# A decoder's routed experts on chosen tokens only: rows scattered by expert, computed in blocks behind the loop, gathered back

## Chip, cores and metric

One core of one Trainium2 chip. The metric is the device time of one execution in microseconds; lower is better. All data are float32 unless a line says otherwise.

## What is computed

Four sequences of 512 tokens of width 256 pass six stages, A to F, each `x = x + stage(layernorm(x))`: five attention layers and, last, the mixture of experts (F), which the change rewrites:

```python
B, S, D_MODEL = 4, 512, 256
E, H, I, G, TKG, TOPK, NSH = 32, 256, 128, 8, 4, 8, 2
scores = sigmoid(h @ gate_w.T); sc = scores + gate_bias
group_scores = top_k(sc.reshape(-1, G, E // G), 2)[0].sum(-1)
masked = where(group in the TKG best, sc, 0); tki = top_k(masked, TOPK)[1]
tkw = take(scores, tki); tkw = tkw / (tkw.sum(-1) + 1e-20) * 2.5
combine = (one_hot(tki, E) * tkw[..., None]).sum(1)          # (tokens, E), 8 of 32 not zero
g = silu(einsum('th,eih->tei', h, w_gate)); u = einsum('th,eih->tei', h, w_up)
routed = einsum('tei,ehi->th', g * u * combine[:, :, None], w_down)
shared = silu(h @ sh_gate.T) * (h @ sh_up.T) @ sh_down.T      # two more experts for all tokens
x = x + routed + shared
```

## The kernel before

The program has a setup and then a loop of four rounds, one per sequence. Each engine has an instruction list of its own; a round runs stages A to F with a barrier of all engines behind each (`Steps.end`), and `end_round` clears the semaphores. x stays in SBUF as four tiles of 128 tokens by 256; SyncE stores it at the end of the round (L2006). TensorE runs warm-up matmuls (`keep_warm`, L412) where it would wait: twelve in front of F's barrier, eight behind.

Stage F (`f_pe`, `f_act`, `f_dve`, `f_sp`) computes all 32 experts for all 512 tokens, with the shared experts as numbers 0 and 1. Per expert `up` (L1257) is four matmuls of 512 columns into two PSUM banks, and `down` (L1286) four of 256 columns that accumulate in banks 6 and 7 over all 34 experts. A float32 matmul stands in the trace as two instructions. Between them ScalarE takes the SiLU (L1332) and VectorE multiplies by the up half (L1378, L1380) and by the token's routing weight (L1387). The routing weights are made by VectorE in `gate` (L1341 to L1371), turned by TensorE and copied through DRAM as one broadcast row per expert (`load_row`, L1223, its source stored at L1230). SyncE loads the experts' weights, 384 KB each, in a ring of six (L1236), and after the sixth the next round's x and the weights of stage A (`load_ahead`, L1215 to L1217). At expert 14 VectorE takes the statistics of the next round's x (L352) and normalises it (L366) in place of `xn`; at experts 18 and 19 TensorE turns it (`next_pe`). At the end VectorE adds banks 6 and 7 to x (L1401).

Of the kernel before, what the change touches and what calls it, by code (L numbers as in the profile page):

```python
# [16 lines left out]
I32 = mybir.dt.int32  # L17
ALU = mybir.AluOpType
# [3 lines left out]
P = 128  # L22
# [168 lines left out]
NRING = 6  # L191
F_ROWS = 4
# [29 lines left out]
def decoder(nc, io, out, rounds=B):  # L222
    ctx = ExitStack()
    with ctx:
# [38 lines left out]
        selE = sb("selE", [96, NE, P], BF16)  # L263
# [23 lines left out]
        x_stored = ctx.enter_context(nc.semaphore("x_stored"))  # L287
        dve_chain = sem("dve_chain")
# [70 lines left out]
        def ln_scaled(dve, ch, rows, powered, n, done):  # L359
# [5 lines left out]
            for i in range(NI):  # L365
                nc.vector.tensor_scalar(xn[:, i, :], rows(i), mv[:, i, 0:1], rstd[:, i:i + 1],  # L366
                                        ALU.subtract, ALU.mult).then_inc(done, 1)

# [30 lines left out]
        def next_pe(pe, k, bank):  # L399
            pe.wait_ge(next_xn, NI)  # L400
            for i in range(NI):
                last = nc.tensor.transpose(ps[:, bank, i * P:(i + 1) * P], xn[:, i, k * P:(k + 1) * P], ident[:, :])
            last.then_inc(next_tr, 1)
# [764 lines left out]
        named("F", "lg_mm", "lg_exp", "comb", "ct_mm", "ct_up", "gu_mm", "silu", "gu", "down")  # L1168

        if "F" in STAGES:  # L1170
            w_in = [sem(f"w_in{k}_F") for k in range(NRING)]


        row_in = [setup_loaded, setup_dve, setup_pool_sem, setup_act]

        F_DIRECT = [NSH, NSH + 1]
        rows_kept = nc.dram_tensor("weight_rows", (NE, S), F32, kind="Internal").ap()

        def row_of(e):

            return ctxT[:, e % F_ROWS // 2, e % 2 * S:(e % 2 + 1) * S]

        F_NEXT_LN = 14
        F_NEXT_T = range(18, 20)

        def f_mem(sb2):
            m = {}
            m["w"] = sb2("f_w", [P, NRING, 3 * DM])
# [4 lines left out]
            m["t8"] = sb2("f_t8", [P, NI, 8])  # L1193
            m["m4"] = sb2("f_m4", [P, NI * 8, 4])
# [5 lines left out]
            m["rest"] = sb2("f_rest", [P, NI, NE])  # L1200
            m["cp"] = sb2("f_cp", [P, NI, 3, NE], BF16)
            m["cT"] = sb2("f_cT", [96, S], BF16)
            m["rows"] = sb2("f_rows", [NE, S])
            m["si"] = sb2("f_si", [P, 2, S])
            m["gu"] = sb2("f_gu", [P, 2, S])
            m["tm"] = sb2("f_tm", [P, S])
# [994 lines left out]
```

## Time and profile before

| | |
|---|---|
| three timed runs, us | 4085.89, 4087.71, 4091.82 (median 4087.71) |
| the profiled execution: span from first to last instruction, us | 4082.7 |
| TensorE / VectorE / ScalarE / POOL busy, us | 3805.6 / 2426.6 / 1752.6 / 152.0 |
| mean granted clock of TensorE | 0.987 |
| DMA: moved, mean rate | 286.26 MB, 70 GB/s |

The page and the trace give the profiled execution's time as its span, 4082.7 us, and no other time of it. An engine's busy time counts no waiting, no register work and no issuing of DMAs. PE is TensorE's matmul side, PEld its weight loads, DVE VectorE, ACT ScalarE, POOL GpSimd, SPq SyncE's queue. A matmul's end is modelled and includes its way through the array, so the distance between starts says what one costs. The granted clock is given in parts of 2.4 GHz.

### The profile page before, as it was taken

The numbers are of one execution on the slowest core, as the hardware profiler recorded it, in microseconds if no ns is written. First come the engines' busy times: TensorE is split into PE (matmuls) and PEld (weight loads), VectorE is DVE, ScalarE is ACT, GpSimd is POOL, SyncE is SP. The second block draws the span as 40 slices with busy tenths as digits, with TensorE's granted clock in tenths as the row PEclk, the third lists the DMA queues.
The fourth block names the chain that finished last, engine by engine and source line by source line (L and its number), as shares of the span: only waits on it lengthen the run. The fifth ranks groups of instructions, "written<-read, shape, count | busy, mean of one in ns | idle before, by whom it ended". The sixth has DMA issues, their size and how long they took to land.

```text
span 4082.7 us, 59517 instructions
## 1 busy us (share of the span) xinstructions
PE 3805.6 (93%) x22502; PEld 1826.4 (45%) x22502; DVE 2426.6 (59%) x6081; ACT 1752.6 (43%) x3256; POOL 152.0 (4%) x168
## 2 busy tenths in 40 slices
PE   4999899999999989999999998999999999899999
PEld 2353444345435244435544524443553443444355
DVE  5568576843366856683237676767333776676642
ACT  1755434531274643462128374336113836433611
POOL 1000020000000002000000001100000000200000
PEclk9999999999999999999999999999999999999999
DMA  5313002133331200203342210130435121012043
GB/s 174 128 43 63 19 17 52 25 111 127 115 119 34 54 19 24 57 13 129 128 137 90 40 38 19 44 50 1 148 109 163 63 52 26 19 46 48 1 164 98
DMA packets 152763, 286.26 MB, mean 70 GB/s; under 512 B 25317, under 2 KB 84709, under 8 KB 147557
## 3 DMA queue, kind: packets, MB, share of 16 engines
q1 hardware_dynamic: 152456, 282.22, 24.1%
q8 instruction: 186, 3.05, 0.3%
q14 instruction: 121, 0.98, 0.1%
HBM read 187.49 MB, written 44.30 MB: 57 GB/s over the span
## 4 chain that ended last, share of the span: by engine, by line
PE 76%; DVE 17%; ACT 4%; issue 2%; PEldq 1%; SPq 0%; DMA 0%; PEld 0%; DVEq 0%; POOLq 0%; ACTq 0%
PE ps L1257 11%; PE ps L589 7%; PE ps L572 6%; PE ps L1286 5%; PE ps L412 5%; DVE mx L755 4%; PE ps L516 4%; PE ps L1676 3%; PE ps L1573 3%; PE ps L577 3%; PE ps L1614 3%; PE ps L468 2%; PE ps L1597 2%; DVE ps L752 2%; PE ps L620 2%
## 5 line engine op out<-in xcount | busy, mean ns | idle before, releaser
L693 ACT ACTIVATE PT<-ps 128x512 f32<-128x512 f32 (+2 forms) x1280 | 643.8, 564 | 324.5 <-PE ps L577 174.7
L1257 PE MATMUL ps<-xnT,f_w 128*128 128x512 f32 x1088 | 489.7, 593 | 0.0
L755 DVE TENSOR_REDUCE mx<-ps 128x1 f32<-128x512 f32 (+3 forms) x768 | 430.7, 617 | 75.4 <-PE ps L516 38.3
L572 PE MATMUL ps<-QS,KS 99*128 99x512 bf16 (+2 forms) x1280 | 419.0, 368 | 9.2 <-ACT PT L693 8.7
L516 PE MATMUL ps<-KS,QS 96*128 96x512 bf16 (+3 forms) x1280 | 391.6, 367 | 17.4 <-DVE mx L755 6.9
L752 DVE CUSTOM_DVE_ANT_0 ps<-ps,mneg 128x512 f32<-128x512 f32 x512 | 340.7, 718 | 82.2 <-PE ps L516 79.1
L589 PE MATMUL ps<-PT,VP 128*32 128x512 f32 (+3 forms) x2560 | 371.1, 573 | 0.0
L412 PE MATMUL ps<-mneg,identb 128*128 128x512 bf16 x1200 | 314.6, 388 | 28.9 <-DVE a_fin L1791 10.9
L1380 DVE TENSOR_TENSOR f_tm<-f_si,ps 128x512 f32<-128x512 f32 x128 | 88.0, 687 | 426.2 <-ACT f_si L1332 425.9
L1332 ACT ACTIVATE f_si<-ps 128x512 f32<-128x512 f32 x136 | 81.3, 597 | 584.2 <-PE ps L1257 584.2
L1257 PEld LDWEIGHTS ps<-xnT,f_w 128*128 128x128 f32 x1088 | 205.5, 190 | 201.4 <-issue 195.2
L572 PEld LDWEIGHTS ps<-QS,KS 99*128 99x128 bf16 x1280 | 108.5, 97 | 390.9 <-ACT PT L693 237.3
L1286 PE MATMUL ps<-f_w,f_gu 128*128 128x256 f32 x1088 | 258.3, 380 | 7.2 <-DVE f_gu L1387 7.2
L1286 PEld LDWEIGHTS ps<-f_w,f_gu 128*128 128x128 f32 x1088 | 205.7, 190 | 93.3 <-issue 59.4
L1791 DVE TENSOR_TENSOR a_fin<-a_fin,ps 128x512 f32<-128x512 f32 (+1 forms) x176 | 104.5, 635 | 208.8 <-PE ps L1656 207.4
L516 PEld LDWEIGHTS ps<-KS,QS 96*128 96x128 bf16 x1280 | 127.5, 100 | 222.5 <-DVE mx L755 73.9
L682 ACT ACTIVATE QS<-ps 3x512 bf16<-3x512 f32 x192 | 113.1, 589 | 225.6 <-PE ps L554 222.5
L1756 ACT ACTIVATE a_X<-ps,b1A 128x1024 f32<-128x1024 f32 (+2 forms) x152 | 169.2, 1156 | 72.1 <-PE ps L1620 71.5
L577 PE MATMUL ps<-mnegT,identb 128*128 128x512 bf16 x512 | 194.6, 380 | 0.0
L412 PEld LDWEIGHTS ps<-mneg,identb 128*128 128x128 bf16 x1200 | 113.1, 100 | 157.5 <-issue 23.2
L775 DVE RECIPROCAL rq<-ps 128x16 f32<-128x16 f32 x48 | 12.4, 257 | 224.8 <-PE ps L526 224.8
L1732 ACT ACTIVATE a_fin<-ps 128x2048 f32<-128x2048 f32 (+1 forms) x64 | 79.2, 1237 | 153.1 <-PE ps L1597 152.4
(282 smaller groups left out, 5584.1 us busy)
## 6 DMA issues: line engine op xcount, KB each, us to landing
f_w<-in_wF SPq DMA_DIRECT2D x136, 384.0 KB, 3.1
ctxT<-weight_rows SPq DMA_DIRECT2D x120, 256.0 KB, 3.4
scores<-a_fin SPq DMA_DIRECT2D x64, 256.0 KB, 3.0
a_fin<-scores SPq DMA_DIRECT2D x32, 512.0 KB, 4.3
a_Y<-in_wA SPq DMA_DIRECT2D x5, 3072.0 KB, 14.7
KS<-KP SPq DMA_DIRECT2D x240, 64.0 KB, 2.3
scores<-a_fin SPq DMA_DIRECT2D x64, 192.0 KB, 3.0
a_fin<-scores SPq DMA_DIRECT2D x12, 1024.0 KB, 7.6
```

The costliest lines, as they stand in the source:

```text
L412: nc.tensor.matmul(ps[:, bank, :], identb[:, :], mneg[:, 0, 0:BANK], start=True, stop=True)
L516: last = nc.tensor.matmul(o, m["QS"][0:KR, h, i * P:(i + 1) * P], m["KS"][0:KR, h, f:f + w], start=True, stop=not c.causal)
L572: last = nc.tensor.matmul(o, m["KS"][0:KST, h, j * P:(j + 1) * P], m["QS"][0:KST, h, q0:S], start=True, stop=plain)
L577: last = nc.tensor.matmul(o, identb[:, :], mnegT[:, j, :], start=False, stop=True)
L589: last = nc.tensor.matmul(ps[r:r + 32, 6, q0:S], m["VP"][:, j, h, :], m["PT"][:, mp % 2, j % 2, e, 0:S - q0], start=(j == 0), stop=(j == c ...
L693: nc.scalar.activation(m["PT"][:, mp % 2, j % 2, e, 0:w], ps[:, SLOTS + n % TURNED, 0:w], ACT.Exp, scale=HD ** -0.5).then_inc(g("exp"), 1)
L752: nc.vector.tensor_tensor_reduce(ps[:, k % SLOTS, 0:w], ps[:, k % SLOTS, 0:w], mneg[:, i, f:f + w], 1.0, NEG, ALU.add, ALU.max, m["mx"][:, ...
L755: nc.vector.tensor_reduce(m["mx"][:, h % 2, i, f // BANK:f // BANK + 1], ps[:, k % SLOTS, 0:w], AX.X, ALU.max, negate=True).then_inc(g("sl ...
L1257: last = nc.tensor.matmul(ps[:, 2 * v + e % 2, :], m["w"][:, e % NRING, (2 * v + k) * P:(2 * v + k + 1) * P], xnT[:, k, :], start=(k == 0) ...
L1286: last = nc.tensor.matmul(ps[:, 6 + i // 2, (i % 2) * DM:(i % 2 + 1) * DM], m["gu"][:, e % 2, i * P:(i + 1) * P], m["w"][:, e % NRING, 2 * ...
L1573: last = nc.tensor.matmul(ps[:, 4 + e % 4, :], m["w"][:, k, col:col + P], xnTA[:, k, :], start=(k == 0), stop=(k == KD - 1))
L1756: nc.scalar.activation(m["hid"][k % 2][:, n * x:n * x + n, 0:w], ps[:, A_UP + n * x:A_UP + n * x + n, 0:w], ACT.Gelu, bias=b1A[:, 0:1]).th ...
```

## The change

In the loop, F computes the gate and the two shared experts only. `chosen` (0 or 1) is counted over the tokens by small bf16 matmuls (`ranks`), so that each chosen (token, expert) pair has a slot: expert number times `ROOM` plus its rank. x with the shared experts added goes to DRAM (`x_kept_rows`); keys and weights of all rounds stay in `hist`. Behind each round's end POOL scatters the 512 normalised rows, eight times each, into `slot_rows` in DRAM. The next round's x is normalised into a buffer of its own (`xnA`) so that `xn` stays for the scatter.

Behind the loop stand new programs of all engines. All 32 experts' weights (12.6 MB) are loaded into SBUF, the tail of each expert's slots is filled with zero rows, and a table of 159 blocks of 128 slots (4 x 512 x 8 pairs, rounded up by expert) is made. Each block is loaded, turned, multiplied with its expert's weights, chosen by a register, and stored. Then POOL gathers each token's eight rows back, and VectorE adds them up with their weights.

```diff
-            for e in range(NE + NSH):
...
-                sp.dma_start(MF["w"][:, e % NRING, :], io["wF"][e]).then_inc(w_in[e % NRING], 16)
-                if e == NRING - 1:
-                    load_ahead(sp, b + 1, ahead)
...
+            for e in range(NSH):
+                sp.dma_start(MF["w"][:, e, :], io["wF"][e]).then_inc(w_in[e], 16)
+            load_ahead(sp, b + 1, ahead)
             sp.wait_ge(ahead, 3 * 16)
...
+            def ranks():
+                pe.wait_ge(g("chosen"), 1)
+                for i in range(NI):
+                    for j in range(i + 1):
+                        nc.tensor.matmul(ps[:, 4, i * NE:(i + 1) * NE], earlierb[:, :] if j == i else onesb[:, :], m["cb"][:, j, :],
+                                         start=(j == 0), stop=(j == i))
+                for i in range(NI):
+                    last = nc.tensor.matmul(ps[:, 4, NI * NE:(NI + 1) * NE], onesb[:, :], m["cb"][:, i, :], start=(i == 0), stop=(i == NI - 1))
+                last.then_inc(g("rank_mm"), 1)
             up(0)
             up(1)
             pe.wait_ge(x_kept, n)
             down(0)
             down(1)
+            ranks()
+            next_pe(pe, 0, 5)
+            next_pe(pe, 1, 1)
...
+            for r in range(B - 1):
+                ch.link(nc.vector.tensor_copy(hist[:, :, NI * r:NI * (r + 1), :], hist[:, :, NI * (r + 1):NI * (r + 2), :]))
...
+            ch.link(nc.vector.tensor_tensor(f2("rp"), f2("rp"), f2("mb"), ALU.is_lt))
+            nc.vector.tensor_copy(m["cb"][:, :, :], f2("rp")).then_inc(g("chosen"), 1)
+            dve.wait_ge(ahead, 3 * 16)
+            ln_stats(ch, lambda i: M1["x"][:, i, :], next_var)
+            ch.link(nc.vector.tensor_tensor(f2("mb"), f2("rp"), f2("sc"), ALU.mult))
...
+            ln_scaled(dve, ch, lambda i: M1["x"][:, i, :], next_pow, 0, next_xn, m["xnA"])
+            dve.wait_ge(g("down"), NSH)
...
+            ch.link(nc.vector.tensor_tensor(key, key, f2("rp"), ALU.mult))
+            for i in range(NI):
+                last = nc.vector.max(m["p8"][:, i, :], hist[:, 0, NI * (B - 1) + i, :])
+            ch.link(last)
+            ch.link(nc.vector.tensor_scalar(slot8[:, :, :], m["p8"][:, :, :], -1.0, None, ALU.add))
...
+        def to_slots(pool):
+            for i in range(NI):
+                for k in range(TOPK):
+                    nc.gpsimd.indirect_dma_start(out=slot_rows, out_offset=bass.IndirectOffsetOnAxis(ap=slot8[:, i, k:k + 1], axis=0),
+                                                 in_=xn[:, i, :], in_offset=None).then_inc(scattered, 16)
...
+        RX, RT, RH, RY, RG = 4, 3, 3, 4, 8
+        NT = B * NI
+        AHEAD_T, AHEAD_U = 3, 2
...
+        def g_sp(sp):
+            for q in range(8):
+                sp.dma_start(m["W"][:, 4 * q:4 * q + 4, :], io["wF"][NSH + 4 * q:NSH + 4 * q + 4].rearrange("e p c -> p e c")).then_inc(g("W_in"), 16)
+            sp.wait_ge(x_stored, 16)
+            sp.dma_start(m["acc"], x_kept_rows.rearrange("b (t p) d -> p (b t) d", p=P)).then_inc(g("kept_in"), 16)
+            sp.wait_ge(g("ends"), 1)
+            for e in range(NE):
+                end = sp.value_load(ends[0:1, e:e + 1], min_val=ROOM * e, max_val=ROOM * e + TOKENS)
+                sp.dma_start(slot_rows[bass.ds(end, P), :], zeros[:, :]).then_inc(g("padded"), 16)
+            sp.wait_ge(g("tables"), 1)
+            sp.wait_ge(scattered, 16 * B * NI * TOPK)
+            sp.wait_ge(g("padded"), 16 * NE)
+            by_block = slot_rows.rearrange("(a p) d -> a p d", p=P)
+            def load(b):
+                if b >= RX:
+                    sp.wait_ge(g("xt_mm"), b - RX + 1)
+                first = sp.value_load(table[b % P:b % P + 1, 1, b // P:b // P + 1], min_val=0, max_val=NE * ROOM // P - 1)
+                sp.dma_start(m["xb"][:, b % RX, :], by_block[bass.ds(first, 1), :, :].rearrange("o p d -> p (o d)")).then_inc(g(f"x_in{b % RX}"), 16)
+            for b in range(RX):
+                load(b)
+            for b in range(NBLOCK):
+                if b + RX < NBLOCK:
+                    load(b + RX)
+                sp.wait_ge(g("y_up"), b + 1)
+                sp.dma_start(block_out[b * P:(b + 1) * P, :], m["y"][:, b % RY, :]).then_inc(g(f"y_out{b % RY}"), 16)
...
+        def g_pool(pool):
+            pool.wait_ge(g("rows8"), 1)
+            for r in range(RY):
+                pool.wait_ge(g(f"y_out{r}"), y_stored(r))
+            for t in range(NT):
+                if t >= RG:
+                    pool.wait_ge(g("summed"), t - RG + 1)
+                for k in range(TOPK):
+                    nc.gpsimd.indirect_dma_start(out=MG["back"][:, t % RG, k, :], out_offset=None, in_=block_out,
+                                                 in_offset=bass.IndirectOffsetOnAxis(ap=rows8[:, t, k:k + 1], axis=0)).then_inc(g(f"back{t % RG}"), 16)
...
+        def g_pe(pe):
+            def turn_x(b):
+                pe.wait_ge(g(f"x_in{b % RX}"), 16 * (b // RX + 1))
+                if b >= 2:
+                    pe.wait_ge(g("xt_up"), b - 1)
+                for k in range(KD):
+                    last = nc.tensor.transpose(ps[:, b % 2, k * P:(k + 1) * P], m["xb"][:, b % RX, k * P:(k + 1) * P], ident[:, :])
+                last.then_inc(g("xt_mm"), 1)
+            def up(b, e):
+                pe.wait_ge(g("xt_up"), b + 1)
+                if b >= 2:
+                    pe.wait_ge(g("hid"), b - 1)
+                for k in range(KD):
+                    last = nc.tensor.matmul(ps[:, 2 + b % 2, 0:2 * P], m["xT"][:, b % RT, k, :],
+                                            m["W"][:, bass.ds(e, 1), 2 * P * k:2 * P * (k + 1)].rearrange("p o c -> p (o c)"),
+                                            start=(k == 0), stop=(k == KD - 1))
+                last.then_inc(g("gu_mm"), 1)
+            def turn_h(b):
+                pe.wait_ge(g("hid"), b + 1)
+                if b >= 2:
+                    pe.wait_ge(g("ht_up"), b - 1)
+                nc.tensor.transpose(ps[:, 4 + b % 2, 0:P], m["h"][:, b % RH, :], ident[:, :]).then_inc(g("ht_mm"), 1)
+            def down(b, e):
+                pe.wait_ge(g("ht_up"), b + 1)
+                if b >= 2:
+                    pe.wait_ge(g("y_up"), b - 1)
+                nc.tensor.matmul(ps[:, 6 + b % 2, 0:DM], m["hT"][:, b % 2, :], m["W"][:, bass.ds(e, 1), 2 * DM:3 * DM].rearrange("p o c -> p (o c)"),
+                                 start=True, stop=True).then_inc(g("y_mm"), 1)
...
+            pe.wait_ge(g("W_in"), 8 * 16)
+            pe.wait_ge(g("tables"), 1)
+            for b in range(-AHEAD_T, NBLOCK):
+                if b + AHEAD_T < NBLOCK:
+                    turn_x(b + AHEAD_T)
+                if b >= 0:
+                    turn_h(b)
+                if 0 <= b + AHEAD_U < NBLOCK:
+                    u = b + AHEAD_U
+                    expert[u] = pe.value_load(table[u % P:u % P + 1, 0, u // P:u // P + 1], min_val=0, max_val=NE - 1)
+                    up(u, expert[u])
+                if b >= 0:
+                    down(b, expert.pop(b))
...
+        def g_act(act):
+            for b in range(-AHEAD_T, NBLOCK):
+                t, u = b + AHEAD_T, b + AHEAD_U
+                if t < NBLOCK:
+                    act.wait_ge(g("xt_mm"), t + 1)
+                    if t >= RT:
+                        act.wait_ge(g("gu_mm"), t - RT + 1)
+                    nc.scalar.activation(m["xT"][:, t % RT, :, :], ps[:, t % 2, 0:DM].rearrange("p (k c) -> p k c", k=KD), ACT.Copy).then_inc(g("xt_up"), 1)
+                if b >= 0:
+                    act.wait_ge(g("ht_mm"), b + 1)
+                    if b >= 2:
+                        act.wait_ge(g("y_mm"), b - 1)
+                    nc.scalar.activation(m["hT"][:, b % 2, :], ps[:, 4 + b % 2, 0:P], ACT.Copy).then_inc(g("ht_up"), 1)
+                if 0 <= u < NBLOCK:
+                    act.wait_ge(g("gu_mm"), u + 1)
+                    if u >= 2:
+                        act.wait_ge(g("hid"), u - 1)
+                    nc.scalar.activation(m["si"][:, u % 2, :], ps[:, 2 + u % 2, 0:P], ACT.Silu).then_inc(g("silu"), 1)
...
+        def g_dve(dve):
...
+            for b in range(-AHEAD_U, NBLOCK):
+                u = b + AHEAD_U
+                if u < NBLOCK:
+                    dve.wait_ge(g("silu"), u + 1)
+                    if u >= RH:
+                        dve.wait_ge(g("ht_mm"), u - RH + 1)
+                    nc.vector.tensor_tensor(m["h"][:, u % RH, :], m["si"][:, u % 2, :], ps[:, 2 + u % 2, P:2 * P], ALU.mult).then_inc(g("hid"), 1)
+                if b >= 0:
+                    dve.wait_ge(g("y_mm"), b + 1)
+                    if b >= RY:
+                        dve.wait_ge(g(f"y_out{b % RY}"), 16 * (b // RY))
+                    nc.vector.tensor_copy(m["y"][:, b % RY, :], ps[:, 6 + b % 2, 0:DM]).then_inc(g("y_up"), 1)
+            dve.wait_ge(g("kept_in"), 16)
+            for t in range(NT):
+                dve.wait_ge(g(f"back{t % RG}"), 16 * TOPK * (t // RG + 1))
+                for k in range(TOPK):
+                    ins = nc.vector.scalar_tensor_tensor(out=m["acc"][:, t, :], in0=m["back"][:, t % RG, k, :], scalar=weight8[:, t, k:k + 1],
+                                                         in1=m["acc"][:, t, :], op0=ALU.mult, op1=ALU.add)
...
         @block.gpsimd
                 st.end_round()
+                to_slots(pool)
+            g_pool(pool)
```

In setup, the table `selE` of POOL goes; two small loads and four fills or copies of VectorE come in.

## Rows read from the trace of the kernel before

**Rows 1.** Busy time of the engines, and the chain that ended last, by engine (the page)

```profile
PE 3805.6 (93%) x22502; PEld 1826.4 (45%) x22502; DVE 2426.6 (59%) x6081; ACT 1752.6 (43%) x3256; POOL 152.0 (4%) x168
...
PE 76%; DVE 17%; ACT 4%; issue 2%; PEldq 1%; SPq 0%; DMA 0%; PEld 0%; DVEq 0%; POOLq 0%; ACTq 0%
```

**Rows 2.** The page's costliest groups, the two of the expert matmuls

```profile
L1257 PE MATMUL ps<-xnT,f_w 128*128 128x512 f32 x1088 | 489.7, 593 | 0.0
...
L1286 PE MATMUL ps<-f_w,f_gu 128*128 128x256 f32 x1088 | 258.3, 380 | 7.2 <-DVE f_gu L1387 7.2
```

**Rows 3.** The chain in order of time, first round, stage F: start us, us, what

```profile
906.04 3.43 PE ps L1257 x8
909.48 1.73 PE ps L1286 x8
```

**Rows 4.** Timeline of stage F, first round: start us, us, instructions [idle before <- releaser]

```profile
864.81 2.71 SPq L1236 DMA_DIRECT2D f_w<-in_wF  x6
...
869.53 1.04 PE L418 MATMUL ps<-ident,xn 128*128 128x128 f32 x8
...
874.12 0.23 DVE L1341 TENSOR_SCALAR f_sc<-f_sc 128x128 f32<-128x128 f32 x1 [3.06 <-ACT f_sc L1319]
...
885.54 0.29 DVE L1360 TENSOR_TENSOR f_rp<-f_rp,f_mb 128x128 f32<-128x128 f32 x1
...
887.25 0.23 DVE L1366 TENSOR_SCALAR f_mb<-f_mb 128x128 f32<-128x128 f32 x1
...
947.77 1.41 DVE L352 BATCH_NORM_STATS2 st<-a_Y 128x6 f32<-128x256 f32 x4
...
1053.70 4.73 PE L412 MATMUL ps<-mneg,identb 128*128 128x512 bf16 x20
1053.97 1.28 DVE L1401 TENSOR_TENSOR x<-x,ps 128x512 f32<-128x512 f32 x2 [2.16 <-PE ps L1286]
```

**Rows 5.** DMA issues: what, engine, count, KB each, median us to landing

```profile
f_w<-in_wF SPq DMA_DIRECT2D x136, 384.0 KB, 3.1
...
KS<-KP SPq DMA_DIRECT2D x240, 64.0 KB, 2.3
...
scores<-a_fin SPq DMA_DIRECT2D x64, 128.0 KB, 2.5
...
wbuf<-in_woA SPq DMA_DIRECT2D x5, 1024.0 KB, 17.1
...
weight_rows<-f_rows SPq DMA_DIRECT2D x4, 64.0 KB, 1.6
```

**Rows 6.** Busy time by stretch, DMA share and GB/s at the right

```profile
874.00:884.00 10.00, 10.00 (x28) 5.12 (x27) 9.29 (x20) 2.57 (x4) 0.00 (x0) 1.00 1.03 409
```

**Rows 7.** SyncE's issues: line, duration ns min/median/max, first and last start

```profile
L1230 SPq DMA_DIRECT2D weight_rows<-f_rows x4: 325/325/330, 892.6 to 3913.2; - x4
...
L2006 SPq FUSED_REGOPS  x4: 42/43/43, 1058.5 to 4079.2; - x4
...
L2006 SPq DMA_DIRECT2D out<-x x4: 404/404/405, 1058.7 to 4079.4; - x4
```

**Rows 8.** Small reads of PSUM and SBUF, by line: duration ns min/median/max

```profile
L424 ACT ACTIVATE xnT<-ps x40: 592/597/619, 301.8 to 3891.8; 128x512 f32<-128x512 f32 x40
...
L366 DVE TENSOR_SCALAR xn<-ps,mv,rstd x64: 529/535/545, 458.7 to 3890.0; 128x256 f32<-128x256 f32 x64
L366 DVE TENSOR_SCALAR xn<-a_Y,mv,rstd x20: 403/407/414, 51.1 to 3980.3; 128x256 f32<-128x256 f32 x20
```

**Rows 9.** Busy time by stretch in stage C; PEclk is the granted clock

```profile
492.00:496.00 4.00, 2.18 (x12) 1.14 (x12) 3.86 (x6) 0.86 (x3) 0.00 (x0) 1.00 0.00 0
...
500.00:504.00 4.00, 2.38 (x7) 0.83 (x7) 3.91 (x5) 2.42 (x6) 0.00 (x0) 0.50 0.01 2
```

**Rows 10.** Timeline of POOL, first round

```profile
294.91 1.01 POOL L390 TENSOR_TENSOR rstd<-mv,half 128x4 f32<-128x4 f32 x1 [244.46 <-DVE mv L357]
```

More of the change, by code:

```diff
@@ L17 @@
 I32 = mybir.dt.int32
+U32 = mybir.dt.uint32
 ALU = mybir.AluOpType
@@ L401, in next_pe @@
             for i in range(NI):
-                last = nc.tensor.transpose(ps[:, bank, i * P:(i + 1) * P], xn[:, i, k * P:(k + 1) * P], ident[:, :])
+                last = nc.tensor.transpose(ps[:, bank, i * P:(i + 1) * P], MF["xnA"][:, i, k * P:(k + 1) * P], ident[:, :])
             last.then_inc(next_tr, 1)
@@ L1390, in f_dve @@
-            gate()
-            for e in range(NSH, NE + NSH):
-                if e == F_NEXT_LN:
-                    dve.wait_ge(ahead, 3 * 16)
-                    ln_stats(ch, lambda i: M1["x"][:, i, :], next_var)
-                product(e)
-                if e == F_NEXT_LN + 1:
-                    ln_scaled(dve, ch, lambda i: M1["x"][:, i, :], next_pow, 0, next_xn)
-            dve.wait_ge(g("down"), NE + NSH)
+                nc.vector.tensor_tensor(m["gu"][:, e, :], m["si"][:, e, :], ps[:, 2 + e, :], ALU.mult).then_inc(g("gu"), 1)
@@ new lines, in f_dve @@
+            ch.link(last)
+            ch.link(nc.vector.tensor_tensor(f2("rp"), f2("rp"), f2("mb"), ALU.is_lt))
[3 more added lines that the diff above has]
+            ch.link(nc.vector.tensor_tensor(f2("mb"), f2("rp"), f2("sc"), ALU.mult))
+            ch.link(nc.vector.tensor_reduce(m["sum"][:, :], f2("mb"), AX.X, ALU.add))
+            ch.link(nc.vector.tensor_scalar(m["sum"][:, :], m["sum"][:, :], 1e-20, None, ALU.add))
@@ new lines, in decoder @@
+        MG = scope(g_mem)
+        flat = MG["W"][:, :, :].rearrange("p e c -> p (e c)")
+        MG["back"] = flat[:, 0:RG * TOPK * DM].rearrange("p (t k c) -> p t k c", t=RG, k=TOPK)
+        MG["acc"] = wbuf[:, :, :].rearrange("p a c -> p (a c)")[:, 0:NT * DM].rearrange("p (t c) -> p t c", t=NT)
+        moe_signals = ("ends", "padded", "tables", "kept_in", "W_in", *(f"x_in{r}" for r in range(RX)), "xt_mm", "xt_up", "gu_mm", "silu", "hid", "ht_mm", "ht_up", "y_mm", "y_up",
+              *(f"y_out{r}" for r in range(RY)), "rows8", *(f"back{r}" for r in range(RG)), "summed", "stored")
@@ new lines, in decoder, with y_stored @@
+        sm.update({("G", signal): s for signal, s in zip(moe_signals, [s for (stage, _), s in list(sm.items()) if stage in "CE"])})
+        def y_stored(e):
+            return [sum(1 for b in range(NBLOCK) if b % RY == r) * 16 for r in range(RY)][e]
+        def g_sp(sp):
+            g = lambda s: sm["G", s]
+            m = MG
+            for q in range(8):
[23 more added lines that the diff above has]
+            for t in range(NT):
+                sp.wait_ge(g("summed"), t + 1)
+                sp.dma_start(out[t // NI, t % NI * P:(t % NI + 1) * P, :], m["acc"][:, t, :]).then_inc(g("stored"), 16)
+            sp.wait_ge(g("stored"), 16 * NT)
@@ L2145, in lay_out_more @@
     part = np.arange(P)[:, None]
+    d["moeC"] = np.tile(np.concatenate([np.arange(NE) * ROOM + 1, np.arange(16) * P, [0, 0]]), (P, 1)).astype(np.float32)
+    d["moeC"][:, NE + 16:] = part + P * np.arange(2)
+    d["tri"] = (part < np.arange(P)).astype(np.float32)
     off = 504 + part // 16 - np.arange(632)[None, :]
```

311 lines of the change are left out of this document (157 added, 154 removed).

## The prediction, on record before any run

> **What bounds the kernel now.** I read the page's shares first, then its chain, then the chain in order of time inside stage F, then what lies around it. TensorE is busy 93% of the span and carries 76% of the chain [rows 1]; POOL works for 152 us in all. The two matmul lines of the experts, L1257 and L1286, are busy for 490 and 258 us [rows 2]. In the chain of stage F one expert is 3.43 + 1.73 = 5.16 us of TensorE without a gap [rows 3], 34 times a round. So stage F is bound by TensorE, and work that leaves it there comes off the end, as long as nothing else takes its place.
>
> The sum is made against the span, 4082.7 us; the median of the three runs, 4087.7, lies 5.0 us above, and I add 5.0 at the end. A measurement of this kernel can tell about 0.2% (8 us) from no change.
>
> **Stage F in the loop.** The first round's F runs from 864.8 to the add of L1401, which ends at 1055.25, and the warm-up matmuls behind it (twelve of the 20 stand before the barrier; 512 bf16 columns stream in 0.215 us, as 256 f32 columns do in 1.73/8 [rows 3]) reach the barrier at 1053.70 + 12 x 0.215 = 1056.3 [rows 4]. In the new F the path is VectorE's. Through the comparison of L1360 its chain is the old one and ends at 885.83 [rows 4]; the three history copies in front of it lie in the 3.06 us in which it waited for the logits [rows 4]. Then: cast 0.23, statistics of the next x 1.41 [rows 4] and some 0.6 for their aggregation, six weight operations 1.6 (L1361 to L1366, 885.87 to 887.48 [rows 4]), three small operations 0.6 (estimated like those), four normalisations of 0.41 [rows 8], add to x 1.28 [rows 4], slots about 1.6 (eight operations of that size): end 894.8. TensorE's shared experts, 14 small rank matmuls and 8 transposes (8 in 1.04 us [rows 4]) lie beside this; its twelve warm-up matmuls end at about 895.5. Saved: 1056.3 - 895.5 = 160.8 us a round, **643 us** in four. The wait for the loads ahead costs nothing: in the old order the last landed 17.1 us after its issue, some 4 us into the stage behind six weight blocks [rows 4, 5], so near 886; now there are two, which at 409 GB/s [rows 6] is 4 us earlier. If it were late, the statistics would be, one for one. The 32 scatters per round are issued by POOL at the start of the next round, where it sits idle for 244 us [rows 10]; even at 2.3 us each they are 74 us and hidden. Setup: +1 us for VectorE's new fills.
>
> **The prelude behind the loop** (nothing covers it). From the last store, 4079.4 [rows 7] less 643 plus 1 = 3437.4. TensorE may not start before 12.6 MB of weights are in: 31 us at 409 GB/s. Beside them run 4.2 MB of scatter, 4.2 MB of zero rows and 2.1 MB of kept rows, 23 MB in all: 57 us at that rate. SyncE issues eight weight loads (~8 us), waits for the store, then 32 times reads a register, computes an address and issues. Issue: 0.33, with a computed address 0.40 + 0.04 [rows 7]. The register read is in no row. Bounds: 0.04, a register operation [rows 7], and 1.6, the shortest round trip of a DMA [rows 5]; it is a round trip without a DMA queue, so I take 0.7. That makes 32 x 1.15 = 37 us behind the first 13, beside 32 indirect DMAs of POOL. I take **60 us**, bounds 45 and 100, and 6 us until the first block is through.
>
> **One block.** TensorE: two transposes, one for h (0.13 each), up 4 instructions and down 2 of 256 columns (0.215 each, from 1.73/8 [rows 3]): 0.39 + 0.86 + 0.43 = 1.7 us, plus its own register read, half hidden by its queue, 0.35: 2.0 us. ScalarE: three reads of PSUM of 256 or 128 columns, about 0.3 each (0.6 for 512), VectorE 0.3 + 0.45 (0.53 for 256) [rows 8]: neither is a bound. But SyncE's program ties loads to stores: behind the load of block b+4 it waits until y of block b is copied, stores it, and only then issues the load of b+5, whose transposes open TensorE's iteration b+2. From the end of iteration b: h of the next block and the copy of y 0.65, store issue 0.33, register read 0.7, address and load until landed, 2.4, wake-up 0.05: 4.15 us, and then iteration b+2 itself, 2.0. The 128 KB landing is between 1.6 (64 KB store) and 3.1 (384 KB load), with 2.3 and 2.5 for 64 and 128 KB [rows 5]; I take 2.3 from issue. So two iterations take 6.15 us, one **3.1 us**, a full 1.1 more than TensorE needs. What the four buffers could hide, the order of SyncE's queue exposes.
>
> TensorE is then idle for a third of the time, and the clock comes in. In stage C, where TensorE was busy 2.18 of 4 us, the granted clock stood at 1.00, and just behind it, with 2.38 of 4, at 0.50, that is 1.2 GHz [rows 9]. At that level its 1.7 us are 3.4, and the loop is (4.15 + 3.4 + 0.35)/2 = 3.9 us a block. No row tells how much of the stage would stand so; between none and all I take a quarter, because all the busier stretches stand at 1.00 [rows 6]: **3.3 us x 159 = 525 us**. Bounds: 2.4 (read 0.04, landing 2.0) and 4.6 (read 1.6, low clock).
>
> For the register read the Trainium skill (DMA: Bandwidth & Descriptors, latency facts) gives a floor of some 600 ns; with 0.6 in place of 0.7 the two iterations would be 0.15 us shorter and the result 12 us lower. No row here shows it.
>
> **The gather.** POOL waits for the last store (3 us), then issues 16 x 8 indirect DMAs of 128 rows. No row has one. Bounds: 0.33, SyncE's issue [rows 7], and 2.3, a DMA issued only when the last has landed [rows 5]. POOL does it in software, and its smallest such operation, a power of 128x4, takes 1.01 [rows 10]: I take 1.1, 128 x 1.1 = **141 us**. VectorE's eight multiply-adds a tile (8 x 0.45 = 3.6) and the stores lie beside it; the last tile adds 8.5.
>
> **Sum** (the old program's last 3.3 us behind its store are in these terms): 3437.4 + 60 + 6 + 525 + 3 + 141 + 8.5 = 4181; plus 5.0 = **4186 us**, 2.4% slower. The loop gives 643 back, and the stage behind it costs 744. It breaks even at (525 - 98)/159 = 2.7 us a block, all else equal.
>
> **Rivals.**
> *TensorE bounds the blocks (faster).* If register reads cost little and a 128 KB load lands in 2 us, two iterations take 0.65 + 0.33 + 0.1 + 0.04 + 2.0 + 1.8 = 4.9, 2.45 a block, with the clock at 1.00 as in stage F: 3.3 - 2.45 = 0.85, x 159 = 135 us less, 4051. For it: the 64 KB store that landed in 1.6. Against: every load in the trace takes 2 us or more. It decides below 2.7 us a block.
> *The clock stays low through the blocks.* 3.9 x 159 = 620, result 4281. For it: the stretch at 0.50 had the same mixture of short transposes, matmuls and idle gaps [rows 9]. Against: at that level such a block is 3.4 of 3.9 us busy, and stretches as busy as that stand at 1.00 [rows 6]. The Trainium skill (TensorE: Matmul & The Clock Gate, HAM oscillation) tells of a kernel in which short bursts of matmuls alternate with waits for DMA and every burst runs at the low clock; by that rule it would be 4281.
> *POOL's indirect DMAs run one by one* at 2.3 us: gather 294, prelude 74: 4186 + 153 + 14 = 4353. For it: no row has POOL issue a DMA at all; against: SyncE issued six in 2.71 us [rows 4].
> *The loop gives less than it says*, because the next round or its scores transfers meet the scatter or a late weight load: up to 20 us a round, 4266.
>
> **How the numbers follow.** My forecast 0.42, TensorE-bound 0.24, low clock 0.14, POOL one by one 0.12, less from the loop 0.08. Faster comes from the second and a bit of the first (cheap reads beside a cheap gather): 0.25. Same (4079.5 to 4095.9): 0.05. Slower: 0.70. The range takes in the TensorE-bound case down to a cheaper gather (0.9 each, 26 us less) and up to the POOL case: 4025 to 4350; the block's upper bound alone would give 4393, whose last part I leave out. The cases on the slow side hold most of the chance; the likeliest one's own range is 4100 to 4270.
>
> **What would show it.** In the changed profile: stage F near 31 us a round; L1257's group at 64 instructions and not 1088; POOL's scatter beside stage A; a stretch of some 60 us with TensorE idle behind the last round; then a period of 3.1 to 3.9 us in which the chain goes through SyncE's issue, DMA and TensorE's first transpose. If the waits before that transpose are short and TensorE is busy throughout, the block step was wrong; if POOL's issues are much above or under 1.1 us, the gather step was; if the granted clock is 1.00 throughout, 0.2 us a block go.

## The result, and the profile of the changed kernel

The changed kernel takes **4253.5 us** (median of 4 runs, 4252.3 to 4257.3) against 4088.2 for the kernel before (4 runs, 4085.9 to 4091.8): ratio 1.0408, 95% interval 1.0393 to 1.0422. It is slower, by 4.1%. The profiled execution took 4253.1 us with a span of 4251.3.

The page of the changed kernel: busy shares, TensorE and its granted clock in 40 slices, and the chain by engine.

```profile
PE 3513.4 (83%) x21913; PEld 1696.6 (40%) x21913; DVE 2442.3 (57%) x6369; ACT 1803.7 (42%) x3597; POOL 388.3 (9%) x420
...
PE   4999899989998999899989998999899944666620
...
PEclk9999999999999999999999999999999977898865
...
PE 61%; DVE 18%; issue 4%; ACT 4%; DMA 4%; SPq 4%; POOL 3%; PEldq 1%; PEld 0%; DVEq 0%; POOLq 0%; ACTq 0%
```

TensorE fell from 93% to 83% of the span and from 76% to 61% of the chain [rows 1]. Where it idles can be seen in the slices: up to the 32nd it is as full as before, then two slices of 4 (the prelude), four of 6 (the blocks), and nearly nothing (the gather). DMA, SyncE's queue and POOL, none of which had a share worth a per cent, now carry 11% of the chain.

The timeline of SyncE's queue across the end of the loop and the prelude, then SyncE's lines of the loop's last store and of the zero rows, then the register read of the block loads (duration in ns min/median/max, first and last start):

```profile
3452.52 0.40 SPq L2174 DMA_DIRECT2D x_kept_rows<-x  x1
3453.16 26.73 SPq L1381 DMA_DIRECT2D g_W<-in_wF  x8
3479.94 5.03 SPq L1383 DMA_DIRECT2D wbuf<-x_kept_rows  x1
3486.02 46.89 SPq L1387 DMA_DIRECT2D slot_rows<-ctxT  x32
3535.31 1.48 SPq L1397 DMA_DIRECT2D g_xb<-slot_rows  x2
...
L2174 SPq DMA_DIRECT2D x_kept_rows<-x x4: 396/400/406, 900.4 to 3452.5; - x4
...
L1387 SPq DMA_DIRECT2D slot_rows<-ctxT x32: 332/332/12394, 3486.0 to 3532.6; - x32
...
L1396 SPq TENSOR_LOAD <-table x159: 263/272/468, 3534.6 to 4068.5; - x159
L1396 SPq FUSED_REGOPS  x159: 152/152/159, 3534.9 to 4068.8; - x159
```

These rows, with the end of the last issue of a store of y (4078.4) and the span's end, cut the time into the prediction's terms:

| stretch | predicted us | measured us | difference |
|---|---|---|---|
| start to the loop's last store | 3437.4 | 3452.5 | +15.1 |
| prelude, to the first load of a block | 60 | 82.8 | +22.8 |
| 159 blocks, with the first one's way through | 6 + 525 | 543.1 | +12.1 |
| gather and end | 3 + 141 + 8.5 | 172.9 | +20.4 |
| span | 4181 | 4251.3 | +70.4 |

So the loop gave back 627 us (4079.4 [rows 7] less 3452.5), and what stands behind it costs 799.

The block stage by stretches of 100 us: busy time of TensorE (count), weight loads, VectorE, ScalarE, POOL, then the granted clock, DMA share and GB/s; and its longest waits.

```profile
3560.00:3660.00 100.00, 64.43 (x264) 45.79 (x263) 18.61 (x58) 24.21 (x88) 0.00 (x0) 0.90 0.25 79
3700.00:3800.00 100.00, 66.78 (x266) 46.89 (x267) 18.60 (x58) 24.06 (x88) 0.00 (x0) 0.90 0.24 78
3900.00:4000.00 100.00, 66.06 (x270) 46.93 (x270) 18.51 (x58) 24.88 (x90) 0.00 (x0) 0.91 0.25 79
```

```profile
PEld ps L1432 <- DMA g_xb<-slot_rows: 168.0, 80, 2.9
...
PE ps L1432 <- DMA g_xb<-slot_rows: 136.4, 77, 2.5
```

No engine is full, and DMA moves 79 GB/s where 409 were seen before [rows 6]. TensorE waits for the rows of a block in about every second block, some 2 us at a time (80 times in the 500 us of 146 blocks). The chain in order of time shows why it is every second one:

```profile
3698.98 0.45 PE ps L1432 x2
...
3699.46 0.39 ACT g_xT L1482
...
3699.97 1.14 PE ps L1440 x4
...
3701.13 0.28 ACT g_si L1492
...
3701.64 0.43 DVE g_y L1563
...
3702.09 0.33 SPq L1405
...
3702.48 0.27 SPq L1396
...
3702.78 0.15 SPq L1396
...
3703.18 1.98 DMA g_xb<-slot_rows
3705.15 0.04 issue
3705.20 0.45 PE ps L1432 x2
...
3706.18 2.07 PE ps L1440 x4
3708.25 0.87 PE ps L1455 x2
```

One turn of this cycle, 3698.98 to 3705.20, is 6.2 us and carries two blocks: transposes of x, ScalarE's copy, the up products, silu, the copy of y; then SyncE stores y (L1405), reads the next block's number (L1396: 0.27 for the load, 0.15 for the address), issues, and 1.98 us later the rows are there. In the next turn the same four instructions of L1440 take 2.07 instead of 1.14 us, because the clock is at its low level for a part of it (0.77 granted between 3705.2 and 3712.7 us, 1.00 in the turn before), and the turn is 7.5 us long.

### The profile page after: what moved, and what is told of

It is laid out like the page before. It is cut to its first block, busy times and chain, and to the rows that moved or that the text cites. A ratio compares the mean times of both kernels' runs of the same rounds, so it can differ in the third digit from the quotient of the medians.

```text
span 4251.3 us, 62126 instructions
## 1 busy us (share of the span) xinstructions
PE 3513.4 (83%) x21913; PEld 1696.6 (40%) x21913; DVE 2442.3 (57%) x6369; ACT 1803.7 (42%) x3597; POOL 388.3 (9%) x420
## 3 DMA queue, kind: packets, MB, share of 16 engines
q14 instruction: 138, 1.13, 0.1%
## 4 chain that ended last, share of the span: by engine, by line
PE 61%; DVE 18%; issue 4%; ACT 4%; DMA 4%; SPq 4%; POOL 3%; PEldq 1%; PEld 0%; DVEq 0%; POOLq 0%; ACTq 0%
PE ps L601 7%; PE ps L584 6%; PE ps L424 5%; DVE mx L767 4%; PE ps L528 4%; DMA g_xb<-slot_rows 4%; PE ps L1843 3%; POOL g_W L1420 3%; PE ps L1440 3%; PE ps L1740 3%; PE ps L589 2%; PE ps L1781 2%; PE ps L480 2%; PE ps L1764 2%; DVE ps L764 2%
## 5 line engine op out<-in xcount | busy, mean ns | idle before, releaser
L1558 DVE TENSOR_TENSOR g_h<-g_si,ps 128x128 f32<-128x128 f32 x159 | 45.8, 288 | 490.6 <-ACT g_si L1492 490.6
L402 POOL TENSOR_TENSOR rstd<-mv,half 128x4 f32<-128x4 f32 x20 | 20.3, 1015 | 2737.9 <-DVE mv L369 2737.9
L1432 PE MATMUL ps<-ident,g_xb 128*128 128x128 f32 x318 | 72.0, 312 | 230.1 <-DMA g_xb<-slot_rows 230.1
L1440 PE MATMUL ps<-g_W,g_xT 128*128 x636 | 206.9, 455 | 37.1 <-ACT g_xT L1482 34.4
L1482 ACT ACTIVATE g_xT<-ps 128x256 f32<-128x256 f32 x159 | 60.9, 383 | 330.0 <-PE ps L1432 329.7
L1420 POOL DMA_INDIRECT g_W<-block_out,rows x128 | 123.9, 968 | 625.8 <-DMA block_out<-g_y 587.1
L1440 PEld LDWEIGHTS ps<-g_W,g_xT 128*128 128x128 f32 x636 | 126.0, 220 | 77.1 <-issue 63.3
L1432 PEld LDWEIGHTS ps<-ident,g_xb 128*128 128x128 f32 x318 | 43.1, 158 | 276.7 <-DMA g_xb<-slot_rows 178.6
```

The lines of the kernel that those rows point to most:

```text
L1420: nc.gpsimd.indirect_dma_start(out=MG["back"][:, t % RG, k, :], out_offset=None, in_=block_out, in_offset=bass.IndirectOffsetOnAxis(ap=row ...
L1440: last = nc.tensor.matmul(ps[:, 2 + b % 2, 0:2 * P], m["xT"][:, b % RT, k, :], m["W"][:, bass.ds(e, 1), 2 * P * k:2 * P * (k + 1)].rearran ...
```

## Experiments

Eleven runs of nine kernels, in three sets, which the recorded texts name calls; the kernels of one set ran on one chip, each set beside the kernel before. The medians of the kernel before were 4087.5 (first set), 4087.6 (second) and 4085.5 (third). The phases named below are read as in the table above.

### First set: SyncE's order, its buffers, its register read, and its zero rows

**e1_order.** SyncE stores y of block b-2, not b, behind the load of b+4:

```diff
-            for b in range(NBLOCK):
+            LAG = 2
+            for b in range(NBLOCK + LAG):
                 if b + RX < NBLOCK:
                     load(b + RX)
-                sp.wait_ge(g("y_up"), b + 1)
-                sp.dma_start(block_out[b * P:(b + 1) * P, :], ...
+                if b >= LAG:
+                    sp.wait_ge(g("y_up"), b - LAG + 1)
+                    sp.dma_start(block_out[(b - LAG) * P:(b - LAG + 1) * P, :], ...
```

> Edit: SyncE's program stores y of block b-2 behind the load of block b+4, where the changed kernel stores y of block b; four x buffers as before. Theory (the order of SyncE's queue sets the block: load b+5 waits behind y of block b, and its transposes open TensorE's iteration b+2): the wait for g_xb goes, a block takes TensorE's own 1.7 to 2.1 us in place of 3.42, the run 210 to 270 us less than the changed kernel: 3985 to 4045. Rival 1 (the transfers themselves, or the DMA rate, set the block): the block stays at 3.2 to 3.5, the run within 30 us of 4254. Rival 2 (TensorE's register read in front of each up sets it): the block stays above 2.6.

**e1_rx8.** The old order, with eight buffers for blocks of x: `RX, RT, RH, RY, RG = 8, 3, 3, 4, 8`.

> Edit: eight x buffers in place of four, the order of loads and stores unchanged. Theory: the load that waits behind y of block b is now that of b+9, needed six iterations later, so the gain is that of the run with the other order, to within 15 us, by another road. Rival (the transfers set the block): within 30 us of 4254.

**e2_two_reads.** A second `value_load` from the table before each block's own; its value is not used.

> Edit: SyncE reads a second register (0.27 us and 0.15 + 0.02 us of register work, some 0.5 with the gaps) in front of each load; nothing uses it. Theory: the loop closes over two blocks and goes through SyncE's read once, so 0.25 us a block, 159 x 0.25 = 40 us more: 4290 (4280 to 4305), a little less if the low clock's share falls. Rival 1 (the loop closes over each block): 80 us more. Rival 2 (SyncE is not on the path): within 8 us of 4254.

**e3_pads_act.** ScalarE issues the 32 stores of zero rows (register read and all) in place of SyncE.

> Edit: the 32 reads and stores of zero rows are issued by ScalarE's queue, which is idle there, and not by SyncE's behind the weight loads. Theory (the 82 us in front of the first block are SyncE's issues in a row: 27 for the weights, 5 for the kept rows, 46 for the zero rows): the blocks begin when POOL's scatter and the weights have landed, 35 to 42 us earlier: 4212 to 4220. Rival (the DMA rate sets this stretch, 23 MB at 300 to 400 GB/s): 0 to 15 us earlier.

The changed kernel's row is the run of the result, from before this set; the ratios are to the kernel before beside each.

| kernel | us (runs) | ratio to before | prelude | blocks, us each |
|---|---|---|---|---|
| changed kernel | 4253.5 (4) | 1.0408 [1.0393, 1.0422] | 82.8 | 3.42 |
| e1_order | 4090.8 (10) | 1.0010 [1.0000, 1.0019] | 83.1 | 1.96 |
| e1_rx8 | 4090.8 (10) | 1.0005 [0.9995, 1.0015] | 83.0 | 1.95 |
| e2_two_reads | 4367.8 (4) | 1.0691 [1.0673, 1.0709] | 84.0 | 3.67 |
| e3_pads_act | 4299.8 (4) | 1.0522 [1.0500, 1.0544] | 63.4 | 3.39 |

In **e1_order** and **e1_rx8** the two ways of loosening load from store do the same thing: a block falls from 3.42 to 1.96 and 1.95 us. At 1.96 us the cycle through SyncE is gone from the chain, and TensorE follows itself. The same kernel in the third set (o2_order_again), chain in order of time, one block and the next one's first four instructions:

```profile
3700.86 1.13 PE ps L1442 x4
3701.98 0.43 PE ps L1457 x2
3702.41 0.22 PE ps L1434 x2
3702.63 0.11 PE ps L1451
3702.74 0.97 PE ps L1442 x4
```

1.13 + 0.43 + 0.22 + 0.11 is 1.9 us. And the clock comes with it, here in e1_rx8, whose SyncE is as in the changed kernel:

```profile
3700.00:3800.00 100.00, 96.72 (x486) 76.90 (x484) 33.17 (x107) 44.25 (x160) 0.00 (x0) 1.00 0.45 143
```

**e2_two_reads** added 0.25 us a block (3.67 against 3.42). The second read, L1397, stands on the chain with the parts of the first:

```profile
3802.96 0.33 SPq L1406
...
3803.35 0.27 SPq L1396
...
3803.65 0.15 SPq L1396
...
3803.90 0.28 SPq L1397
...
3804.22 0.15 SPq L1397
...
3804.61 2.07 DMA g_xb<-slot_rows
```

That is some 0.55 us with the gaps, once for two blocks. So a read on this path costs about 0.27 us a block, and SyncE's queue does lie on the cycle, once for two blocks as forecast.

**e3_pads_act** shortened the prelude by 19.4 us, to 63.4 (3517.65 to 3581.03): less than the theory's 35 to 42 and more than the rival's 15. What is left is the data: with two queues the DMA engines are at 1.01 and 0.98 of their time in the prelude's two halves and move 376 and 374 GB/s.

In all four, though, the loop itself ended late: its last store stood at 3509.7 to 3517.7, not at 3452.5, although no edit touches the loop. That is 57 to 65 us which these totals hold and the first profile does not. Mainly for this reason the totals of e1_order, e2_two_reads and e3_pads_act lie above their forecasts, while e1_rx8 equals e1_order as expected; the delay hides most of the gain of e1_order and turns e3's into a loss. In rounds 2 to 4, stage A, the one beside the scatter, took 222 to 231 us in place of 205 to 207; in round 1, with no scatter beside it, it took 206 to 207. The waits of its second round, 906 to 1130 us, in e1_order, then its third round by the timeline:

```profile
ACT a_fin L1901 <- remote: 37.7, 3, 20.9
```

```profile
1789.00 2.00 PE L1766 MATMUL ps<-a_X 32*128 32x512 f32 x16
...
1813.76 1.88 ACT L1901 ACTIVATE a_fin<-ps 128x2048 f32<-128x2048 f32 x1 [39.85 <-remote]
1815.69 2.94 PE L1766 MATMUL ps<-a_X 32*128 32x384 f32 x16 [22.78 <-ACT a_fin L1901]
```

"Remote" says that the profile found no instruction that released the wait. In the changed kernel's first profile the same three waits of round 2 are for TensorE and 22.3 us long (19.1, 1.7 and 1.5). By kernel.py it is TensorE's scores (L1766) that ScalarE waits for here too: L1901 copies them out of PSUM, and for the first group of heads, to which all of these copies belong, it waits for nothing else; the wait for stores of scores stands behind `if hq`. In round 3 above TensorE's matmuls have their (modelled) end at 1791.0, and ScalarE starts 22.8 us later; in o2_order_again, the same file, it starts 0.06 us after them. TensorE then waits for ScalarE in turn. The recorded theory of the next set, stores of scores held up behind the scatter's packets, does not fit these waits. Whether the matmuls or only their signal came late can't be told, as their ends are modelled. In round 2 of all four kernels and rounds 3 and 4 of e1_order, the last such wait ended 1 to 4 us behind the end of the scatter's last issue (945.15 and 942.1 in e1_order's round 2). So two questions were open: is the delay the kernels' own, and is it the scatter's doing?

### Second set: the changed kernel again, the scatter, the gather, the clock

**c1_again.** The changed kernel, no edit.

> The changed kernel once more, no edit, beside the kernel before on the chip of this call. The four experiments so far all left the loop 60 to 65 us later than the first profile of the changed kernel, although their edits lie behind the loop: stage A of rounds 2 to 4 took 222 to 231 us instead of 205 to 207. Theory of the run (the delay is not of the kernels' making, the scatter's packets and the score stores of stage A share the DMA engines and fall out differently from one place of the buffers or one chip to another): this run too shows 222 to 231 us and about 4310 us in all. Rival (the edits moved the loop's code or its buffers): 205 to 207 us and 4254 us.

**s2_late_scatter.** e1_order, and POOL issues the scatter of a round inside stage A of the next round:

```diff
...
-        EXTRA["A"] = dict(pe=a_pe, act=a_act, dve=a_dve, pool=lambda *_: None, sp=a_sp)
+        def a_pool(pool, *_):
+            pool.wait_ge(sm["A", "v_up"], 8)
+            to_slots(pool)
+
+        EXTRA["A"] = dict(pe=a_pe, act=a_act, dve=a_dve, pool=a_pool, sp=a_sp)
...
                 st.end_round()
-                to_slots(pool)
+            to_slots(pool)
             g_pool(pool)
```

The rows' slots are first filled with rows 2048 to 2175 of each expert's room, so that round 1's empty scatter hits nothing that is read.

> The kernel in which SyncE stores y two blocks late, and the scatter of a round's rows is issued inside the next round's stage A, after the last value projection is read out (some 65 to 75 us into the stage, when nearly all score stores are issued) instead of at its start; the last round's scatter stays right behind the loop. A first, empty scatter into rows that nothing reads goes with round 1. Theory (score stores held up behind the scatter's packets): the waits of ScalarE and VectorE on DMAs early in stage A vanish, stage A goes back to 205 to 208 us in rounds 2 to 4, time 4090 - 60 = 4030 us. Rival 1 (the score loads of the later part of stage A are held up instead): the loss moves, stage A stays over 215 us in all four rounds, time 4090 to 4110 us. Rival 2 (the scatter has nothing to do with it): stage A stays at 222 to 231 us in rounds 2 to 4 and 206 in round 1, 4090 us.

**g1_half_gathers.** The gather's loop over k runs to 4, and VectorE waits for four. The kernel leaves out half of each token's rows, so its output is not the decoder's; it serves for the time alone.

> The changed kernel with only the first four of each token's eight result rows gathered (64 indirect DMAs of 128 rows instead of 128); the sum still runs over eight buffers, four of which hold other data. Theory (each indirect DMA costs GpSimd 0.96 us plus 0.30 us to the next, whatever the transfers do): the last phase shrinks from 163 to 82 us, 81 us less than the same kernel with all gathers run in this call. Rival (VectorE's weighted sums of 4.15 us a tile, or the landing of the rows, set the pace): with four gathers of 1.26 us = 5.05 us a tile against 4.15 us the pace is still GpSimd's, but a floor of 16 x 4.15 = 66 us is near; if rows land late, less than 60 us is gained.

**w1_warm.** Three matmuls of 384 bf16 columns, into the unused part of a PSUM bank, ahead of the wait in front of a block's transposes.

> The changed kernel with three dummy matmuls of 384 columns before each block's transposes of x, where TensorE waits for the block's rows. Theory (the block is bound by the chain through SyncE's queue, over two blocks, in which TensorE's work at the low clock takes part: 2.07 instead of 1.03 us for one block's first products): the clock stays at 1.00, TensorE's share of the chain shrinks, and a block falls from 3.42 to 3.1 us, 50 us less than the same kernel in this call. Rival A (the clock costs little, since the queue and the landing are most of the chain): under 15 us less. Rival B (the dummy matmuls, 0.5 us a block, delay the transposes that the chain waits for): 20 to 80 us more.

| kernel | us (4 runs each) | ratio to before | loop's last store | prelude | blocks, us each | gather and end |
|---|---|---|---|---|---|---|
| c1_again | 4250.3 | 1.0398 [1.0375, 1.0420] | 3451.0 | 83.1 | 3.38 | 173.0 |
| s2_late_scatter | 4025.9 | 0.9843 [0.9823, 0.9864] | 3455.3 | 82.6 | 1.96 | 173.2 |
| g1_half_gathers | 4172.3 | 1.0200 [1.0180, 1.0220] | 3449.7 | 82.9 | 3.43 | 92.9 |
| w1_warm | 4227.8 | 1.0343 [1.0321, 1.0365] | 3451.6 | 83.2 | 3.22 | 172.5 |

No kernel of this set shows the delay, whether edited behind the loop (g1, w1) or not (c1, which was expected at 4310). So an edit behind the loop does not bring it by itself; that e1_order's does not, the third set shows. And s2_late_scatter could not show what it was made for: without a delay there was nothing to take away.

**g1_half_gathers**: 64 gathers fewer save 78 us by the medians and 80 in the phase, 1.25 us each. POOL's issue sets the pace. The rows of L1420, of g1:

```profile
L1420 POOL DMA_INDIRECT g_W<-block_out,rows x64: 942/946/1204, 4081.0 to 4162.4; - x64
...
  issue: 19.2, 63
...
  DVE wbuf L1568: 24.7, 16
```

0.946 us each and 19.2/63 = 0.30 to the next; VectorE waits for them before every tile, even at four per tile.

**w1_warm** gained 22 us on c1_again, between the theory's 50 and the rival's 15. The clock stood at 0.98 to 1.00 where c1_again had 0.88 to 0.92, and TensorE's dummy work fills part of its idle time:

```profile
3700.00:3800.00 100.00, 76.54 (x372) 52.11 (x372) 19.30 (x62) 25.71 (x93) 0.00 (x0) 1.00 0.26 83
```

Blocks took 511.3 us instead of 537.7. The clock's part of the blocks is thus at least 26 us of the 225 us between the two orders of SyncE (the dummy matmuls may hide a bit more); the rest, at most 199 us, is the cycle's.

### Third set: the order again, and the parts together

**o2_order_again** is e1_order's file once more, **s3_late_again** that of s2_late_scatter.

> The kernel in which SyncE stores y two blocks late, once more. In the first call (four kernels on one chip) stage A of rounds 2 to 4 took 222 to 231 us in every kernel, in the second call (another chip) 205 to 207 in every kernel whose scatter is where the change puts it, edits behind the loop or not. Theory (the score stores wait behind the scatter's packets on some chips and not on others): where stage A takes 205 to 207 us here, this kernel takes about 4029 us, where it takes 222 to 231, about 4090 us. Rival (the edit of SyncE's order itself lengthens stage A): 4090 us and 222 us or more, whatever the other two show.

> SyncE's order as above, and the scatter issued inside the next round's stage A, once more, beside the kernel without that. Theory: 4025 us on any chip; where the kernel above takes 4029 us, the two agree within 5 us, and the late scatter is worth something on the other chips alone. Rival (the late scatter gains by itself): 20 us or more under the kernel above on any chip.

**b1_all.** On s2_late_scatter: zero rows of experts 0 to 17 by ScalarE, 18 to 31 by SyncE, and the load of the kept rows moved behind them.

```diff
-            sp.wait_ge(x_stored, 16)
-            sp.dma_start(m["acc"], x_kept_rows...)
             sp.wait_ge(g("ends"), 1)
-            for e in range(NE):
+            for e in range(18, NE):
                 end = sp.value_load(ends[0:1, e:e + 1], ...)
                 sp.dma_start(slot_rows[bass.ds(end, P), :], zeros[:, :])
+            sp.wait_ge(x_stored, 16)
+            sp.dma_start(m["acc"], x_kept_rows...)
...
+            act.wait_ge(g("ends"), 1)
+            for e in range(18):
+                end = act.value_load(ends[0:1, e:e + 1], ...)
+                act.dma_start(slot_rows[bass.ds(end, P), :], zeros[:, :])
```

> The best of the parts together: y stored two blocks late, scatter inside the next round's stage A, the zero rows split (18 experts on ScalarE's queue, 14 on SyncE's behind the weights), and the load of the kept rows moved behind them. Theory (the prelude is the longer of the queues): SyncE 26.7 + 14 x 1.45 = 47 us, ScalarE 6 + 18 x 1.76 = 38 us, GpSimd's last scatter 41 us and its landing: the blocks start about 48 us behind the loop's last store instead of 82, 34 us less: 3991 us. Rival (the weights' loads, 12.6 MB, which the split does not shorten, or their landing of 23 us set the start): prelude of 60 us or more, over 4003 us.

| kernel | us (4 runs each) | ratio to before | loop's last store | prelude | blocks, us each |
|---|---|---|---|---|---|
| o2_order_again | 4020.7 | 0.9839 [0.9823, 0.9856] | 3450.2 | 82.8 | 1.96 |
| s3_late_again | 4023.4 | 0.9843 [0.9826, 0.9860] | 3453.1 | 82.7 | 1.97 |
| b1_all | 4002.3 | 0.9796 [0.9780, 0.9813] | 3449.7 | 58.0 | 1.97 |

The same file took 4090.8 in the first set and 4020.7 here, with the block stage alike (1.96 us) and the loop's end 61 us apart; the waits on "remote" are gone from stage A. Another 6.6 us of the 70 lie outside the profiled span: the time is 8.0 to 8.8 us above the span in every run of the four kernels of the first set, and 1.7 to 2.1 in all others, the kernel before in that same set among them. The delay is of the execution's surroundings, not of the kernel's text. The late scatter gains nothing where there is no delay; whether it would help where there is one was not seen. b1_all beats both kernels: 2.0% under the kernel before. Its time lies between the theory's 3991 and the rival's 4003, close to the rival. Its prelude is 58.0 us, ten more than the queues' own sum: the data set it, as the rival had it, though 2 us below the rival's 60. By stretches, the prelude of the changed kernel and, behind it, that of b1_all:

```profile
3452.00:3484.00 32.00, 0.25 (x2) 0.00 (x0) 23.73 (x62) 0.00 (x0) 24.12 (x25) 0.57 0.98 371
3484.00:3500.00 16.00, 0.00 (x0) 0.00 (x0) 0.00 (x0) 0.00 (x0) 7.50 (x8) 0.50 1.04 402
3500.00:3534.00 34.00, 0.00 (x0) 0.00 (x0) 0.00 (x0) 0.00 (x0) 0.00 (x0) 0.50 0.47 157
```

```profile
3450.00:3485.00 35.00, 0.00 (x0) 0.00 (x0) 23.38 (x62) 0.00 (x0) 26.74 (x27) 0.54 1.02 381
3485.00:3505.00 20.00, 0.00 (x0) 0.00 (x0) 0.00 (x0) 0.00 (x0) 5.45 (x6) 0.50 1.03 397
```

In the changed kernel the last 34 us run at 157 GB/s; in b1_all the DMA engines are full up to 3505 us, 2.7 us before the first load of a block.

## Why the prediction was right, and where its sizes were off

The sign and the forecast's mechanism held: stage F gave back what it should, and the blocks behind the loop ran at the pace of SyncE's queue. The time was 67 us, 1.6%, above the forecast, still inside its own range, and every stretch of the table came out longer than the sum had it, by 12 to 23 us. No luck was needed for the total, since the misses do not cancel; inside the block's cycle they do.

- **The loop: 627 of 643 us.** F's path in the first round went down from 193.9 us (865 to 1059) to 34.7, 159.2 saved where the sum had 160.8; in rounds 2 and 4 it was 35.7. One thing missed is TensorE's clock at F's end: with the expert matmuls gone it works there only now and then (2.5 of 8 us from 884 to 892), the granted clock from 892 to 896 us is 0.50, and eight transposes like those that took 1.04 us [rows 4] take 1.97, in the second line here (timeline of TensorE, changed kernel):

```profile
870.41 1.04 PE L430 MATMUL ps<-ident,xn 128*128 128x128 f32 x8
...
892.55 1.97 PE L414 MATMUL ps<-ident,f_xnA 128*128 128x128 f32 x8 [4.94 <-DVE f_xnA L378]
894.31 5.78 PE L424 MATMUL ps<-mneg,identb 128*128 128x512 bf16 x20
```

  F makes 635 of the 643; the other 8 us are spread over the other stages. That the scatter is hidden in stage A was right in this profile (205 to 207 us beside it, 206 in round 1 without it), and wrong in the first set's runs, where the rival "the loop gives less" came true with 57 to 65 us in all, against its 80.
- **The prelude: 83, not 60.** The step that failed is "23 MB in all: 57 us" taken beside "32 x 1.15 = 37 us", as if the longer of the two counted. They came one after the other. SyncE's issues themselves took long while the large loads were under way: the eight of the weights, put at some 8 us, took 26.7 (the last one 10.4), the kept rows' 5.0, and the first zero rows' 12.39 (the maximum of L1387 above), to 3498.4. Only then did the other 31 zero rows go out, at 1.09 us each, 34 us with the DMA engines half empty. The price of an item was nearly right (1.15); its place was not. e3_pads_act and b1_all, with a second queue for them, took 63.4 and 58.0.
- **The block: 3.42, not 3.3.** The forecast's two-block cycle of 6.15 us at full clock is 6.2 on the chain. That it fits so well is partly luck, because its errors cancel: the register read is 0.5 with its gaps (3702.48 to 3702.99) and not 0.7, and the landing 2.0 and not 2.3; against that the way from landed rows to the copied y is 3.1 us (0.45 + 0.39 + 1.14 + 0.28 + 0.43 with the hand-overs between engines), more than the 2.0 + 0.65 of the sum. The clock, guessed at a quarter of the stage at 1.2 GHz, was granted 0.90 on average, a fifth at the low level; a turn that meets that level is 7.5 us.
- **The rival "TensorE bounds the blocks"** did not occur, but its place was right: when the order of SyncE's queue is loosened a block is 1.96 us, and the kernel is faster than before by 1.6%. The break-even of 2.7 us a block lies between: from 3.42 to 1.96 us is 231 us for 159 blocks (543.1 less 312.3), and the measured step is 233 (4253.5 to 4020.7).
- **The rival "the clock stays low"** did not occur: 0.90, not 0.50. The Trainium skill (TensorE: Matmul & The Clock Gate, HAM oscillation) tells of bursts that all run at the low clock when waits for DMA lie between them; here waits of 2 us lie between bursts of 4, and of the 140 blocks counted between 3560 and 4060 us 30 have their up products at the low level (2.07 us). w1_warm shows what that is worth, some 26 us.
- **The gather: 1.25 us a DMA, not 1.1.** 0.946 for the instruction and 0.30 to the next one: the second part was not in the sum. 128 of them are 162 us. The rival "one by one, at 2.3" fell: a gather lands in 2.8 us, and the next is issued 1.25 us after it.
- The Trainium skill's figure for a register read (DMA: Bandwidth & Descriptors, Latency and other measured facts), some 0.6 us, is above what this trace shows, 0.27 for the load and 0.15 for the address; the trace decides.

## What to carry to other kernels

When one queue issues both loads ahead and stores of results, ask which result each load stands behind: here four buffers of look-ahead were worth two, since the load of block b+5 waited for y of block b, and two lines of order were worth 233 us (four more buffers made the blocks as fast). Where a stretch moves much data and issues many small DMAs on one queue, add the two times unless the small ones have a queue of their own. And an indirect DMA of 128 rows of 1 KB costs GpSimd 1.25 us here; at 128 in a row with nothing beside them, that is 162 us, the next thing to take away.

## What was not expected of the hardware

The four kernels of one set each lost 57 to 65 us in stage A and those of the two other sets nothing, one file among them being the same in both, while the kernel before took the same time in all three (4087.5, 4087.6, 4085.5). It is the stage beside which GpSimd scatters (1536 packets, 4.2 MB), and it is lost only in the rounds that have a scatter beside them, in hand-overs from TensorE to ScalarE and VectorE that came up to 22.8 us late where they take 0.06 us in the same file otherwise. Its cause is open: the runs exclude the edits and do not name what differs. The chip's number alone does not, since the first and the third set are on record with the same one, 13. That the scatter is needed for the delay is argued from the rounds and from the end of the waits; no run without it, or with it elsewhere, was made under the delay. Such a thing would have been taken for an effect of the edit, had the kernel not been run again.
